# Cross-attention: the normalised tile x2 computed by VectorE instead of GpSimd

## The reference, cut to what matters

```
x  = layernorm(x + L0_attn(x))
logits  = einsum(q, k) + bias            # 16 heads of 32, q = x, k = v = ctx
weights = softmax(logits / sqrt(32))
x  = layernorm(x + combined(weights, v) @ w_out)      # this x is called x2 below
x  = layernorm(x + ffn(x))               # ffn quantises x by amax = max(|x2|)
layernorm(x) = (x - mean) / sqrt(var + 1e-5)
```

## Time and profile before

| | |
|---|---|
| runs, median (lowest, highest) | 2305.74 us (2298.34, 2331.83), 3 runs |
| profiled execution, its own time | 2303.44 us |
| its span | 2301.7 us |
| busy share of the span | PE 91%, DVE 75%, ACT 47%, POOL 37% |
| self-attention stage, 0 to 560 us | DVE busy 407.12 us, PE 493.59 us |
| cross-attention stage, 560 to 1306 us | DVE busy 614.32 of 746 us, PE 704.18 us, POOL 378.55 us |
| feed-forward, first part, 1306 to 1833 us | DVE busy 317.55 us, PE 456.54 us |
| feed-forward, second part, 1833 to 2301 us | DVE busy 391.83 us, PE 444.76 us |

### The profile page before, as it was taken

How to read it: one execution, slowest core, us unless ns; L and a number is a source line. 1 busy time by engine, 2 the same in 40 slices (tenths; PEclk the granted TensorE clock), 3 DMA queues, 4 the chain that set the end, 5 groups by cost and what they waited for, 6 DMA issues and landing times. The chain is left out here.

```text
span 2301.7 us, 32961 instructions
## 1 busy us (share of the span) xinstructions
PE 2099.1 (91%) x11904; PEld 1162.5 (51%) x11904; DVE 1730.8 (75%) x3281; ACT 1081.3 (47%) x1522; POOL 842.9 (37%) x819
## 2 busy tenths in 40 slices
PE   7999999984999999998999468899999599999997
PEld 3444444431777776776777233344444244444443
DVE  6768686865787897997998365966665488888885
ACT  1444444442555554554555133344444465555551
POOL 3122221322154555555555532222222134444442
PEclk9999999996798998998999779999999899999999
DMA  6344342457789889979974278788888457667762
GB/s 231 108 136 143 103 147 100 119 132 186 199 191 216 224 187 209 239 189 208 242 160 113 74 224 276 233 271 269 269 275 272 194 205 230 232 224 230 232 223 81
DMA packets 386947, 448.53 MB, mean 195 GB/s; under 512 B 279463, under 2 KB 279751, under 8 KB 368353
## 3 DMA queue, kind: packets, MB, share of 16 engines
q1 hardware_dynamic: 322736, 286.14, 45.4%
q0 software_dynamic: 64048, 160.28, 22.5%
HBM read 259.00 MB, written 138.73 MB: 173 GB/s over the span
## 5 line engine op out<-in xcount | busy, mean ns | idle before, releaser
L1656 PE MATMUL ps_h<-xT,w 128*128 128x512 f16 x2048 | 453.4, 384 | 22.7 <-ACT h L1487 12.7
L1896 PE MATMUL ps<-w,g_hi 128*128 128x512 f16 x1024 | 389.3, 380 | 28.4 <-DVE g_lo L1834 28.4
L1896 PE MATMUL ps<-w,g_lo 128*128 128x512 f16 x1024 | 389.3, 380 | 0.0
L1656 PEld LDWEIGHTS ps_h<-xT,w 128*128 128x128 f16 x2048 | 201.7, 99 | 268.6 <-issue 18.7
L1487 ACT ACTIVATE h<-ps_h,b_in_sb,col_scale 128x512 f32<-128x512 f32 x256 | 197.7, 777 | 262.8 <-PE ps_h L1656 235.6
L1225 PEld LDWEIGHTS ps_o<-vm,pT 128*128 128x128 f32 x2048 | 293.4, 199 | 13.2
L1059 DVE TENSOR_REDUCE stack<-ps_m 128x2 f16<-128x308 f32 x512 | 243.8, 478 | 59.6 <-PE ps_m L1179 47.6
L1225 PE MATMUL ps_o<-vm,pT 128*128 128x33 f32 x2048 | 279.9, 262 | 0.0
L1017 ACT ACTIVATE pT<-logit 128x512 f32<-128x512 f32 x320 | 198.7, 624 | 113.8 <-DVE logit L1077 112.8
L1749 POOL TENSOR_TENSOR rstd<-vare,minus_half 128x1 f32<-128x1 f32 x64 | 154.2, 2410 | 212.0 <-DVE vare L1852 212.0
L1563 DVE TENSOR_REDUCE amax_t<-h 128x1 f32<-128x2048 f32 x64 | 146.2, 2284 | 102.5 <-ACT h L1487 101.6
(11 more groups left out here) (175 smaller groups left out, 3840.2 us busy)
## 6 DMA issues: line engine op xcount, KB each, us to landing
hidden<-h POOLq DMA_DIRECT2D x64, 1024.0 KB, 6.7
hT<-hidden SPq DMA_DIRECT2D x64, 1024.0 KB, 6.0
xc<-x_cols SPq DMA_DIRECT2D x16, 1024.0 KB, 5.1
xr<-x_rows SPq DMA_DIRECT2D x16, 1024.0 KB, 5.4
x_rows<-x POOLq DMA_DIRECT2D x16, 1024.0 KB, 4.8
x1t<-x_rows SPq DMA_DIRECT2D x64, 256.0 KB, 3.7
bt_main<-bias_main SPq DMA_DIRECT2D x16, 1024.0 KB, 6.6
xres<-x_rows SPq DMA_DIRECT2D x64, 256.0 KB, 4.0
```

The costliest lines, as they stand in the source:

```text
L1656: mm = pe.matmul(ps_h[f % 4][:], w1[:, c, f * P:(f + 1) * P], xT[:, e, a, :, c, :], start=(a == 0 and c == 0), stop=(a == 1 and c == KC - 1))
L1896: mm = pe.matmul(ps[t][:], g[:, e, f, t * P:(t + 1) * P], w2[:, f, :], start=(f == 0 and a == 0), stop=(f == FC - 1 and a == 1))
```

## The change

`finish` moves from POOL to DVE. On DVE it runs at k=2 of the quarter with offset -7, behind `add_bias(2)`. It waits for the root of the same tile, for the store of the tile two before, and for the magnitude of that tile. `magnitude` moves from k=6 with offset -8 to k=4 with offset -7, which is the same quarter as `finish`. POOL keeps `combined_low`, `reciprocal_root`, and, under the name `store`, the wait for x2 and its store; the spacer is gone. ACT, PE and SP are the same as before.

```
-            def finish(s, b, t):
+            def store(s, b, t):
                 ...
                 tile = 4 * (4 * s + b) + t
                 e = t % 2
-                pool.wait_ge(rstd_ready, tile + 1)
-                if not (isinstance(tile, int) and tile < 2):
-                    pool.wait_ge(x2_out[e], 16 * (2 * (4 * s + b) + t // 2))
-                    pool.wait_ge(amax_part, tile - 1)
-                pool.tensor_tensor(spacer[:], minus_half[:], minus_half[:], ALU.mult)
-                pool.tensor_scalar(x2t[:, e], y[:, e], mv[:, e, 0:1], rstd[:, e:e + 1],
-                                   ALU.subtract, ALU.mult).then_inc(x2_ready, 1)
                 pool.wait_ge(x2_ready, tile + 1)
                 pool.dma_start(x2_rows[b]...[bass.ds(s, 1), t]..., x2t[:, e]).then_inc(x2_out[e], 16)
...
                 combined_low(*span_at(s, b, i, -2))
                 reciprocal_root(*span_at(s, b, i, -7))
-                finish(*span_at(s, b, i, -7))
+                store(*span_at(s, b, i, -7))
                 low_half(*span_at(s, b, i, 6))
...
+            def finish(nu, t):
+                if not inside(nu, t):
+                    return
+                tile = 4 * nu + t
+                e = t % 2
+                dve.wait_ge(rstd_ready, tile + 1)
+                if tile >= 2:
+                    dve.wait_ge(x2_out[e], 16 * (2 * nu + t // 2))
+                    dve.wait_ge(amax_part, tile - 1)
+                dve.tensor_scalar(x2t[:, e], y[:, e], mv[:, e, 0:1], rstd[:, e:e + 1],
+                                  ALU.subtract, ALU.mult).then_inc(x2_ready, 1)
...
                     if k == 5:
                         normalise(*at(n, i, -1), 0)
-                    if k == 6:
-                        magnitude(*at(n, i, -8))
+                    if k == 2:
+                        finish(*at(n, i, -7))
+                    if k == 4:
+                        magnitude(*at(n, i, -7))
```

More of the change, by code:

```diff
@@ L694, in cross_attention_stage @@
         amax_run = sb("amax_run", [P, 1], F32)
-        spacer = sb("spacer", [P, 1], F32)
         ps_m = [ctx.enter_context(nc.psum_tensor(f"ps_m{i}", [P, 512], F32)) for i in range(2)]
```

## The result

The changed kernel takes 2543.35 us (median of 6 runs, 2539.51 to 2556.21) against 2307.62 us before (6 runs): a ratio of 1.1042, 95% interval 1.1009 to 1.1076. It is slower by 236 us. The forecast was 2516 us, the range 2432 to 2635.

What follows compares the result with a forecast made beforehand. PE was taken to bound the steady quarter, busy all 10.33 us, with DVE following; 170 (stall) + 68 (clock) + 7 - 4 - 30 gave +211 us on the profiled 2303.44 us, stated as 2516 us, range 2432 to 2635.

Steps and rivals of the forecast that it cites:

- The loop: DVE's finish waits for POOL's root, whose chain leads back through ACT to DVE's add_bias(2): 3.06 us waiting per quarter.
- The work: On DVE, the moved operation takes 0.47 us per quarter, which fits into some 0.77 us of slack.
- rival C: At finish, k=2: the new wait is covered, not slower, about 2302 us; chance 0.05.
- path through maximum(5): DVE's steps up to maximum(5) delay PE's block 7 and y: 3.27 us more per quarter, 13.60 instead of 10.33.
- The clock: PE's 2.83 us idle lowers its granted clock in one quarter of three, 4.0 us each: 68 us over 52 quarters.
- The stretched quarters: Quarters 7 to 58 lengthened by ACT's wait for the transposed stack: of 42 us, 30 come back.
- The ends: Quarters 59 to 63 cost 7 us for all; the drain saves 4 us as POOL's x2 leaves the last chain.
- A: Quarters 7 to 58: the stall without falls of the clock, 2448 us; chance 0.26.
- B: Quarters 7 to 58: the clock falls in nearly every quarter, 2656 us; chance 0.15.
- D: The stall is real but worth less, or the long quarters pay more: 2350 to 2430 us; chance 0.06.

Runs made afterwards that it cites:

- experiment 1: Changed kernel with two POOL lines swapped, the root computed before combined_low: 2307.01 us, ratio 0.9998.
- experiment 2: Changed kernel with finish on DVE at k=6 and magnitude at k=7 instead of k=2 and k=4: 2309.44 us, ratio 1.0003.
- experiment 3: Kernel before, x2 still on POOL, with only a DVE wait at k=2 for the tile's root: 2465.38 us, ratio 1.0693.
- experiment 4: Kernel before with one more DVE operation of x2's form at k=2, on its own buffer, without a wait: 2302.78 us, ratio 0.9984.
- experiment 6: Changed kernel with finish at k=4 and magnitude at k=6 on DVE: 2339.70 us, ratio 1.0138.
- experiment 5: Changed kernel with 14 unused matmuls on PE before max_pair(5), filling its idle time: 2447.89 us, ratio 1.0607.
- experiment 9: Changed kernel with 5 unused matmuls on PE before max_pair(5): 2470.33 us, ratio 1.0705.
- experiment 7: Kernel before with one ACT swap, exponential 4 taken before the two stack halves: 2302.96 us, ratio 0.9979.

## Why the prediction was right

**The loop.** Right in mechanism and size. A DVE wait of 3.06 us was worked out from ACT's and POOL's rows, 2.97 us was measured, 52 times; PE's idle time before block 5 was to be 2.83 us and is 2.63; the quarter without a fall is 13.60 us, as worked out. Experiments 1 and 2 open the loop from either side and the loss is gone; experiment 3 makes the loss with nothing but the wait.

**The work.** Right: 0.47 us in 0.77 us of slack costs nothing (experiment 4). That is also what occupancy sees, and why it misled: rival C needed the root 3.0 us earlier, and experiment 1, which supplies just that, takes no longer than the kernel before, as rival C has it. Behind the wait the slack is used up, and there DVE's work counts: of the 3.27 us, 2.4 come with the wait alone (experiment 3) and 0.9 with x2 and the magnitude behind it. The prediction's path through maximum(5) has both in it.

**The clock.** Right in kind, too small in number. I took a fall in one quarter of three at 4.0 us each, 68 us for 52 quarters. Measured: 24 falls in 52 quarters, which come in pairs of 16.6 + 14.1 = 30.7 us; two undisturbed ones would be 27.2, so 3.5 us a fall, 84 us together. The term that was mis-sized is the frequency, 0.46 instead of one third; the price was a little lower than forecast, and a quarter with a fall takes 16.6 us, not 17 to 18. That only 1.9 us idle are left behind a fall was forecast, and 1.92 to 1.95 were measured. Such a stretch never brought a fall here, in 24 cases, while the one behind a quarter at full clock, 2.63 us in most, did in 24 of 28. With that alternation the share is nearly one half. The Trainium skill, TensorE: Matmul & The Clock Gate, section HAM oscillation, describes a kernel whose clock falls once for every tile since each brings an idle stretch; here the second tile of each pair escapes. That it does so because its idle stretch is shorter, 1.92 us, is likely but not shown: in experiment 3 stretches of 1.98 us did bring falls.

**The stretched quarters.** Right in direction; I took back 30 us of 42, and all of them are gone: 170 (52 x 3.27) + 84 - 42 = 212 us. Of the 42, some 17 were falls of the clock already: quarters 12, 27 and 45 of the kernel before take 16.1, 15.7 and 16.5 us at a mean clock of 0.67 to 0.69, each behind a stretched quarter. The stretched quarters are back wherever the stall is gone or short (experiments 1, 2 and 6) and away where it stands (3, 5 and 9), so it is the stall that removes them. How it does so I had argued (ACT asks later for the transposed stack), and that is not shown: experiment 7 makes ACT's wait hold up less in another way and wins nothing. In quarters 7 to 58 the core's DMA rate fell from 206 to 151 GB/s, so transfers that meet less other traffic are a rival that no run tests.

**The ends.** I gave +3 us. From quarter 59 to the last store it was 18.7 us, with the clock at 0.79 instead of 0.97. In these quarters there is no maximum to hand over, yet x2 waits 2.98 us all the same, quarters 59 to 61 take 10.0 to 10.3 us instead of 8.4, and at the low clock quarter 62 takes 14.8 us instead of 8.9.

**The errors together.** Against the sum of 211 us the clock was 16 us more, the ends 16 more, the rest of the kernel 2 more, and the stretched quarters gave back 12 more: 233 us, which is the difference of the profiles without the start of the stage. So an error of 34 us was partly hidden by one of 12 the other way, and this part is luck. The other 5 to 6 of the 27 us by which the forecast was low are the difference between the profiles and the medians.

**Rivals.** A, no falls, would have been 2448 us; experiment 5 is that case, made on purpose, at 2447.89; that the two agree so closely is luck, since A's sum has the same errors of the ends and of the stretched quarters, and the kernel before took 2312.86 us beside experiment 5. B, a fall in every quarter, 2656 us, stayed out. For D, a smaller stall, nothing was found.

## What to carry to other kernels

Before an operation is moved to another engine, follow its inputs back through every engine's program order: if the chain comes back to an instruction that stands just in front of the new place, the whole latency of the chain becomes a stall in each iteration, and no busy share shows it. Here the same move costs 10% or nothing depending on which of two neighbouring lines of a third engine comes first. And price a stall of TensorE twice, by its length and by what the clock may add. Work that is free where an engine has slack counts again once it stands behind a wait.

## What was not expected of the hardware

- PE's idle time before block 5 and falls of the clock, counted over quarters 7 to 58: at 0.35 to 1.18 us none (experiments 5 and 6); at 1.75 to 1.78 us none of 12 (experiment 9); at 1.96 to 2.00 us 5 of 32 in experiment 9, but 7 of 11 in experiment 3; at 2.17 to 2.30 us 25 of 34 (experiment 3); at 2.63 us and more, in nearly every quarter that began at full clock (quarters 11 to 13 of the changed kernel escaped, and quarter 14 with 2.41 us). Elsewhere in the stage a stretch of 1.42 us that ACT ended brought one (experiment 4, PE's start at 777.20 us), while one of 1.52 us before did not the earlier trace rows. What decides stays open.
- How long a fall lasts differs too. In the changed kernel it keeps PE at 1.2 GHz for some 10 us; in experiment 3 most quarters with a fall take 14.4 us at a mean clock of 0.88, so they are over much sooner.
- Useless matmuls in a stall of the engine bought back 95 us, 4% of the kernel.
- The start of the stage scatters by 20 us between executions of kernels whose work up to there is the same (quarter 7 at 650 to 670 us); in the two that were looked at, the granted clock in it was 0.74 and 0.61.
